# Attention of a decoder layer written out without loops, with its per-round steps made once and its sums on GpSimd

## The reference

```
q = (x @ Wq + bq) * 1/sqrt(16);  k, v = split(ctx @ Wkv + bkv)
q = fq_sym(q, -1); k = fq_sym(k, -1); v = fq_sym(v, axis of tokens)
attn = softmax(q @ k^T)                     # per head, 2048 keys
attn = fq_unsigned(attn, -1)                # s = max(attn)/255; round(attn/s) * s
out  = (attn @ v) @ Wp + bp
```

## Time and profile before

| what | us |
|---|---|
| median of 3 runs | 2234.46 |
| lowest, highest run | 2227.49, 2244.91 |
| the profiled execution, its own time | 2242.98 |
| its span from first to last instruction | 2241.2 |
| mean granted TensorE clock in it | 0.941 |
| attention stage in it | 1202 to 2046 |

### The profile page before, as it was taken

One profiled execution on the slowest core, in us unless ns is written; L12 is line 12 of the kernel. 1 busy time (PEld: TensorE's weight loads), 2 busy tenths in 40 slices (PEclk: granted clock), 3 DMA queues, 4 the chain that ended last, 5 costly groups with the idle time before them and its releaser, 6 DMA issues. The chain is left out here.

```text
span 2241.2 us, 42040 instructions
## 1 busy us (share of the span) xinstructions
PE 1832.4 (82%) x12368; PEld 1273.1 (57%) x12514; DVE 1682.5 (75%) x2852; ACT 1673.6 (75%) x2987; POOL 527.5 (24%) x433
## 2 busy tenths in 40 slices
PE   6888999999999999999676667666676666664999
PEld 5776878777777777777453322222222222232887
DVE  5885676867777777777886888888878887886443
ACT  4667888888888888888368888888888887895211
POOL 2002555555555555555100000000000000002001
PEclk8998999999999999999899998899888998997999
DMA  4000000000000000000814998888888887896000
GB/s 133 15 5 29 0 28 0 28 0 28 0 28 0 28 0 28 0 28 0 174 26 83 167 166 156 154 164 164 160 152 160 161 163 150 161 166 145 10 10 19
DMA packets 566191, 173.18 MB, mean 77 GB/s; under 512 B 535168, under 2 KB 558592, under 8 KB 566144
## 3 DMA queue, kind: packets, MB, share of 16 engines
q1 hardware_dynamic: 566144, 172.57, 38.1%
HBM read 27.83 MB, written 2.10 MB: 13 GB/s over the span
## 5 line engine op out<-in xcount | busy, mean ns | idle before, releaser
L1278 ACT ACTIVATE levels<-s_ps,nb,qstep 128x512 int16<-128x512 f32 (+1 forms) x768 | 696.8, 915 | 118.8 <-DVE nb L1215 115.4
L1145 PE MATMUL s_ps<-kT,qT 128*128 128x512 bf16 x1451 | 492.0, 429 | 266.6 <-ACT levels L1278 253.4
L1204 DVE TENSOR_REDUCE mx<-s_ps 128x1 f32<-128x512 f32 (+1 forms) x768 | 636.6, 864 | 69.0 <-PE s_ps L1145 49.6
L603 DVE SCALAR_TENSOR_TENSOR xs<-x_ps,cw,xs 128x508 f32<-128x508 f32 (+2 forms) x393 | 291.1, 741 | 174.3 <-ACT xs L525 135.9
L1145 PEld LDWEIGHTS s_ps<-kT,qT 128*128 (+1 forms) x1532 | 117.7, 101 | 513.8 <-issue 488.5
L494 PE MATMUL o_ps<-wo,hid 128*128 x1024 | 242.9, 380 | 4.9 <-DVE acc L590 4.9
L659 POOL TENSOR_TENSOR hid<-y,sg 128x512 f32<-128x512 f32 x128 | 175.4, 1371 | 277.5 <-ACT sg L547 184.8
L1505 POOL MEMSET minus_half_o<- 128x4 f32 x1 | 0.1, 102 | 962.8 <-POOLq L1087 962.8
L494 PEld LDWEIGHTS o_ps<-wo,hid 128*128 128x128 f32 x1024 | 192.7, 189 | 39.5 <-issue 9.8
L1155 PEld LDWEIGHTS ao_ps<-vi,levels_T 128*128 128x128 f16 x4096 | 145.7, 98 | 82.7 <-issue 35.9
L525 ACT ACTIVATE xs<-x_ps,cb,cw 128x512 f32<-128x512 f32 x131 | 101.8, 777 | 116.5 <-PE x_ps L446 116.4
(11 more groups left out here) (200 smaller groups left out, 3220.5 us busy)
## 6 DMA issues: line engine op xcount, KB each, us to landing
w_raw<-winT_dram SPq DMA_DIRECT2D x18, 512.0 KB, 4.4
wo_raw<-woutT_dram SPq DMA_DIRECT2D x9, 512.0 KB, 5.7
kT<-zeros SPq DMA_DIRECT2D x4, 1024.0 KB, 19.4
qT<-zeros SPq DMA_DIRECT2D x4, 1024.0 KB, 16.0
levels_T<-levels SPq DMA_TRANSPOSE x256, 4.3
acc<-xT_dram SPq DMA_DIRECT2D x4, 512.0 KB, 6.1
w_bc<-winT_dram SPq DMA_DIRECT2D x16, 128.0 KB, 2.4
acc<-x_dram SPq DMA_DIRECT2D x1, 2048.0 KB, 11.5
```

Of the source, the lines that this page charges most:

```text
L603: dve.scalar_tensor_tensor(to, x_ps[:, :, 0:SEQ - s], cw[:, head, TAPS - 1 - s], to, ALU.mult, ALU.add).then_inc(chain if s < TAPS - 1 els ...
L1145: return pe.matmul(s_ps[:, BANKS[h % 2][chunk], :], qT[:, bass.ds(round_, 1), h % NH, :].rearrange("p b t -> p (b t)"), kT[:, h % NH, at:a ...
L1204: dve.tensor_reduce(mx[:, h % 2, at:at + 1], src, AX.XY if what == "cd" else AX.X, ALU.max).then_inc(max_done, 1)
L1278: act.activation(levels[:, s, at:at + banks * GT].rearrange("p (c k) -> p c k", c=banks), s_ps[:, bank:bank + banks, :], ACT.Exp, bias=nb[ ...
```

## The change

All engines' streams of `attention` are written out for the 256 units; no `Fori`, no register, no `held` is left in it (other stages keep theirs). The order of the work on PE, ACT and SP stays. `steps` is done once, at the start, for all 16 rounds (three instructions over 128 x 256 instead of 16 times three over 128 x 16). The two additions and the inversion of a round's sums go to GpSimd, which gets a block, with a power of -1 for the reciprocal; `sums` and `rtot` keep two rounds. DVE keeps the product with `rtot`. ACT waits for `tot_ready` before it overwrites sums.

```diff
-        nstep = sb("nstep", [P, NH])
-        shift = sb("shift", [P, NH])
+        nstep = sb("nstep", [P, BATCH, NH])
+        shift = sb("shift", [P, BATCH, NH])
-        sums = sb("sums", [P, BATCH, NH, 3])
-        rtot = sb("rtot", [P, NH])
+        sums = sb("sums", [P, 2, NH, 3])
+        minus_one = sb("minus_one", [P, NH])
+        rtot = sb("rtot", [P, 2, NH])
...
-        def rounds(eng, body):
-
-            body(0)
-            with eng.Fori(1, BATCH - 1) as qt:
-                body(qt)
-            body(BATCH - 1)
...
+            for n in range(UNITS):
+                s = n % RING
+                sp.wait_ge(cd_exp, n + 1)
+                if n >= RING:
+                    sp.wait_ge(pv_done, n - RING + 1)
+                sp.dma_start_transpose(lT[:, s, :, :].bitcast(F16), levels[:, s, :].bitcast(F16)).then_inc(turned[s], 16)
...
+            for n in range(UNITS):
+                if n + 1 < UNITS:
+                    pe.wait_ge(a_exp, n + 1)
+                    score(n + 1, "a").then_inc(a_ready, 1)
+                if n + 2 < UNITS:
+                    pe.wait_ge(b_exp, n + 1)
+                    for _ in range(2):
+                        score(n + 2, "b")
+                    score(n + 2, "b").then_inc(b_ready, 1)
+                if n >= LAG:
+                    if n % NH == LAG and n >= NH:
+                        pe.wait_ge(scaled, n // NH)
+                    values(n - LAG)
+                if n + 2 < UNITS:
+                    pe.wait_ge(cd_exp, n + 1)
+                    score(n + 2, "c")
+                    score(n + 2, "d").then_inc(cd_ready, 1)
...
+            def finish(qt):
+
+                dve.wait_ge(tot_ready, qt + 1)
+                dve.wait_ge(pv_done, (qt + 1) * NH)
+                dve.tensor_tensor(att[:, qt, :].rearrange("p (h d) -> p h d", h=NH),
                                   o_ps[:, 0:E].rearrange("p (h d) -> p h d", h=NH),
+                                  rtot[:, qt % 2, :].unsqueeze(2).to_broadcast([P, NH, HD]), ALU.mult).then_inc(scaled, 1)
...
+            dve.tensor_scalar(nstep[:, :, :], qstep[:, :, :], -1.0, None, ALU.mult).then_inc(step_chain, 1)
+            dve.wait_ge(step_chain, 1)
+            dve.reciprocal(shift[:, :, :], nstep[:, :, :]).then_inc(step_chain, 1)
+            dve.wait_ge(step_chain, 2)
+            dve.tensor_scalar(shift[:, :, :], shift[:, :, :], LN255, None, ALU.mult).then_inc(step_chain, 1)
+            dve.wait_ge(step_chain, 3)
+            for n in range(UNITS):
+                maxima(n, "b")
+                if n % NH == LAG + 1 and n >= NH:
+                    finish(n // NH - 1)
+                maxima(n, "cd")
+                maxima(n, "a")
+                bias(n)
+            finish(BATCH - 1)
...
+            for n in range(UNITS):
+                act.wait_ge(nb_ready, n + 1)
+                if n % NH == 0 and n >= 2 * NH:
+                    act.wait_ge(tot_ready, n // NH - 1)
+                if n >= RING:
+                    act.wait_ge(turned[n % RING], n // RING * 16)
+                exps(n, "a", a_exp)
+                exps(n, "b", b_exp)
+                exps(n, "cd", cd_exp)
...
+        @block.gpsimd
+        def _(pool):
+            pool.memset(minus_one[:, :], -1.0).then_inc(chain, 1)
+            for qt in range(BATCH):
+                at = qt * 2 + 1
+                pool.wait_ge(cd_exp, (qt + 1) * NH)
+                if qt >= 2:
+                    pool.wait_ge(scaled, qt - 1)
+                pool.wait_ge(chain, at)
+                pool.tensor_tensor(part[:, :], sums[:, qt % 2, :, 0], sums[:, qt % 2, :, 1], ALU.add).then_inc(chain, 1)
+                pool.wait_ge(chain, at + 1)
+                pool.tensor_tensor(tot[:, :], part[:, :], sums[:, qt % 2, :, 2], ALU.add).then_inc(chain, 1)
+                pool.wait_ge(chain, at + 2)
+                pool.tensor_tensor(rtot[:, qt % 2, :], tot[:, :], minus_one[:, :], ALU.pow).then_inc(tot_ready, 1)
```

More of the change, by code:

```diff
@@ L1157, in values @@
                 mm.then_inc(pv_done, 1)
[L1159 to L1181, removed]
@@ L1195, in _, with maxima @@
+            for n in range(UNITS - LAG, UNITS):
+                values(n)
         @block.vector
         def _(dve):
-            def maxima(n, h, what):
-                bank = BANKS[h % 2]
+            def maxima(n, what):
+                u = n % 2
+                bank = BANKS[u]
                 ready, at, src = {"b": (b_ready, 0, s_ps[:, bank["b"], :]),
@@ L1249, in body @@
-            def body(qt):
-                for h in range(NH):
-                    n = qt * NH + h
-                    if exists(qt, h, 1):
-                        maxima(n + 1, h + 1, "b")
-                    if h == NH - 1 and exists(qt, h, 1):
-                        steps(qt + 1)
-                    if h == LAG and exists(qt, 0, -1):
-                        finish(qt, qt - 1)
-                    if exists(qt, h, 1):
-                        maxima(n + 1, h + 1, "cd")
-                        maxima(n + 1, h + 1, "a")
-                        bias(n + 1, h + 1)
@@ L1263, in _ @@
-            steps(0)
-            maxima(0, 0, "b")
-            maxima(0, 0, "cd")
-            maxima(0, 0, "a")
-            bias(0, 0)
-            rounds(dve, body)
-            finish(BATCH, BATCH - 1)
+            def finish(qt):
+                dve.wait_ge(tot_ready, qt + 1)
+                dve.wait_ge(pv_done, (qt + 1) * NH)
+                dve.tensor_tensor(att[:, qt, :].rearrange("p (h d) -> p h d", h=NH),
+                                  o_ps[:, 0:E].rearrange("p (h d) -> p h d", h=NH),
+                                  rtot[:, qt % 2, :].unsqueeze(2).to_broadcast([P, NH, HD]), ALU.mult).then_inc(scaled, 1)
@@ L1271, in _, with exps @@
+            finish(BATCH - 1)
         @block.scalar
         def _(act):
-            def exps(n, qt, h, what, done):
-                u, s = h % 2, h % RING
-                banks = len(what)
-                at, bank = KEYS[u][what[0]], BANKS[u][what[0]]
+            def exps(n, what, done):
+                u, s = n % 2, n % RING
+                qt, h = divmod(n, NH)
+                first = min(what, key=lambda c: BANKS[u][c])
+                banks, at, bank = len(what), KEYS[u][first], BANKS[u][first]
@@ L1277, in exps @@
                 k = "abc".index(what[0])
                 act.activation(levels[:, s, at:at + banks * GT].rearrange("p (c k) -> p c k", c=banks),
-                               s_ps[:, bank:bank + banks, :],
-                               ACT.Exp, bias=nb[:, u:u + 1], scale=qstep[:, bass.ds(qt, 1), h],
-                               accum_out=sums[:, bass.ds(qt, 1), h, k:k + 1].rearrange("p q s -> p (q s)")
-                               ).then_inc(done, 1)
-            def body(qt):
-                for h in range(NH):
-                    n = qt * NH + h
-                    act.wait_ge(nb_ready, n + 1)
-                    if exists(qt, h, -RING):
-                        act.wait_ge(turned[h % RING], qt * (16 * NH // RING) + h // RING * 16)
-                    exps(n, qt, h, "a", a_exp)
-                    exps(n, qt, h, "b", b_exp)
-                    exps(n, qt, h, "cd", cd_exp)
@@ L1294, in _ @@
-            rounds(act, body)
+                               s_ps[:, bank:bank + banks, :], ACT.Exp, bias=nb[:, u:u + 1], scale=qstep[:, qt, h:h + 1],
+                               accum_out=sums[:, qt % 2, h, k:k + 1]).then_inc(done, 1)
+            for n in range(UNITS):
[7 more added lines that the diff above has]
+                exps(n, "cd", cd_exp)
```

99 lines of the change are left out of this document (27 added, 72 removed).

## The result

The changed kernel takes **2146.97 us** (median of 4 runs, 2145.85 to 2148.35) against 2235.36 for the kernel before beside it: ratio 0.9603, 95% interval 0.9565 to 0.9641. The direction and the place were forecast, the size was not: 2167 with a lower end of 2150. The profiled execution took 2146.56 us, its span 2144.8. In it `attention` lasts from 1202 to 1950 us instead of 1202 to 2046.

The account below looks back on a forecast made before the run. Bound: attention's per-unit chain of ACT, PE and DVE, with ACT waiting for DVE's bias. Terms -82.2 + 2.0 + 7.5 - 0.7 = -73.4 us gave 2169.6 from the profiled execution; forecast 2167 us, own range 2155 to 2180, with rivals 2150 to 2195.

Parts of the forecast that it names:

- (1): All attention units written out run at round 0's 2.932 us per unit from unit 2 to unit 255: -82.2 us.
- (3): DVE keeps only the multiplication of `finish` each round, 0.5 us 15 times: +7.5 us (1.7 to 24).
- (2): `steps` done once for 16 rounds on DVE, ahead of the first maxima: +2.0 us, bounds 1.5 to 2.4.
- (4): Sums and power go to idle GpSimd; DVE's additions and reciprocal fall away at the stage's end: -0.7 us.
- (5): SyncE issues the same 256 transposes in order, its waits now on constants: nothing gained or lost.
- A: GpSimd's power blocks DVE's bias instruction `low` through shared ports: 9 to 21 us, about 2182 us; chance 0.12.
- B: TensorE's clock still falls once a round, set off by the multiplication alone: +16.5 us, 2184 us; chance 0.14.
- C: Written-out code streamed through the transposes' DMA queues stalls an engine, PE above all: 225 us, 2392 us; chance 0.03.
- D: 2.93 holds for some units only; transposes pile up and the turn becomes 3.00: +18 us, 2185 us; chance 0.11.

## Why the prediction was right and wrong

Right: only the attention stage moved, the chain ACT, PE, DVE sets its turn, the written-out rounds are faster, and the falls of the clock go (0.99). Forecast in all -73.4 us, measured -96.4. By its own steps:

- **(1) Writing out, forecast -82.2.** This is the step that failed. It took the 2.932 of round 0 for all units and said "a balance that I don't expect to be better than there". But rounds 0 and 15 still carried `held`, and the diff takes it out. The measured turn is 2.873; 253 x 0.059 = 14.9 us. Giving `held` back restores 2.932 and costs 16.4 us. The sign of it stood in the trace: DVE's `low` waited 0.19 us behind each maxima. The difference between "written out before" and "written out after" was never listed edit by edit; a stretch of the same trace is evidence only for the instructions that it has. The 14.9 us alone would leave the time at 2152, inside the range; with the 7.5 us of (3) it falls below the lower end of 2150.
- **(2) Steps once, forecast +2.0, bounds 1.5 to 2.4.** Measured +1.14 up to unit 2, below both. The old three were put at 0.58 us, the sum of their lengths; from the start of the first to the next maxima they took 1.04 (1.03 in the earlier trace rows), the new ones 2.44, so +1.4 at DVE. The reciprocal took 1.75 us (1.76 forecast); the two tensor_scalar took 0.29 each, not the 0.41 of a row with other operands.
- **(3) `finish`, forecast +7.5, bounds 1.7 to 24.** It cost nothing, less than the lower bound. The slack between "b" and "cd" was read as the 0.24 us that the row calls a wait; from start to start it is 0.93 us with the product or without. The product starts 0.60 us behind the start of "b", so 0.33 us are free, and its 0.33 fits. No clock fall follows. (The whole of `finish`, back on DVE, costs 15.9 us: what is left of it on DVE decides.)
- **(4) GpSimd, forecast -0.7.** Measured -0.14: PE's last products waited for their transposes, as before, and came 0.5 us later behind unit 255. Cover for the power was there; its 2.91 us end at 1302.59, DVE wants it at 1308.17.
- **(5) SyncE, forecast nothing**: 256 transposes that land after 4.6 us; nothing seen.

The errors add up: 14.9 + 7.5 - 0.9 (a few disturbed units: 727.8 against 253 x 2.873) = 21.5 in the turn, +0.9 at the start, -0.6 at the end, 1.3 outside the stage; 23 in all.

The rivals: **A** (the power blocks the bias) fell. `low` at 1301.67 lies inside the power (1299.68 to 1302.59) and takes 0.22 us as always (its 256 instances have a mean of 222 ns). So it does in all 15 rounds in which the power meets a `low`, 2.0 us after the power's start. The Trainium skill (SBUF — State Buffer, section "SBUF: two separate sides") has whichever came first hold the shared ports for its whole instruction; by that, an estimate from the two rows, `low` would have waited 0.9 us, to the power's end. The trace disagrees for this pair, and the measurement decides; for large tiles stand. **B** (the clock still falls once a round) fell: 0.99. It wasn't wrong as a mechanism, since with three small delays together it cost 19 us. That scores take "twice as long" at the lower clock isn't in the earlier trace rows; the three of "b" took 1.44 instead of 0.81 us, 1.8 times. **C** (instruction stream) fell: 63 blocks on q8 and 42 on q14 over the execution (28 and 19 before), the DMA share at 105% in the stretch, and no idle time that belongs to them. The Trainium skill (Runtime: NRT & Kernel Launch, section "Instruction fetch mechanics") expects just that of a straight stream, and the trace agrees. **D** (2.93 doesn't hold) fell: the turn held, lower still, while DMA moved 181 GB/s instead of 159.

What the change gave, by the experiments: about 32 us for the loop, 16 for `held`, 16 for `finish`, 9 for the steps (4, and 5 for their increments), and about 19 for the falls of the clock that these together brought. These sum to 92; measured were 88 to 94, by which runs of before one takes. Of the loop's cost the profiles show where it lies (its turn, and 0.07 us in each unit); which of the register's uses, targets or addresses, makes the 0.07 was not tested.

## What to carry to other kernels

A stretch of the same trace that "already runs the new way" is the best evidence there is, but list first what the diff removes from that stretch too: an increment that does no work cost 0.03 us at one place and 0.11 at another, and six of them per unit made the turn 0.059 us longer, 256 times over. Such a cost is paid only where the engine has no wait to hide it: one increment on DVE lengthened every second unit. Where engines meet in a chain with little slack, single delays add up until PE's idle time lets TensorE's clock fall, and then the price grows (20 us here beyond the sum of the parts); measure them together as well as singly. After such a change read again which wait is left: here it was one of 0.24 us, and splitting one reduction in all units, not only where the wait showed, gave 16 us more.

## What the runs showed of the hardware

- A semaphore increment between a wait and its instruction isn't free: 0.03 us for one on DVE (`low` 0.17 instead of 0.14 us behind the maxima), 0.05 for two, and 0.11 for each of three between the step instructions (0.70 instead of 1.03 us without them). Two on DVE and four on PE per unit cost 16.4 us over 256 units.
- A low granted clock and PE's idle time can keep each other up: with idle times of 1.29 us every 6.8 us on PE the clock was 0.75 on the mean of a whole round; two matmuls of 256 columns in that idle time brought the stretch from 0.91 to 0.98 and 19 us back.
- Scores that are computed and thrown away are worth 54 us here: without them the clock stays at 0.50 and a score shows as 0.61 instead of 0.38 us.
- A power on GpSimd over 128x16 takes 2.91 us and did not delay a VectorE instruction with two small SBUF inputs (128x3) that started within it, in 15 rounds out of 15.
- A loop over all engines cost some 32 us for 14 turns: 0.64 us at each turn and 0.07 us in each of the other units, by the profiles.
